# The experts' down products of a mixture-of-experts kernel, each made as two matmuls of 256 columns in place of one of 512

## The reference, cut to what matters

```python
xn = _layernorm(x, axis=-1)
x = x + _L0_attn_ref(xn, ...) + _L0_ffn_ref(xn, Wg, w1, w2)
```

```python
dispatched = xr[dispatch_mask.reshape(-1) % S].reshape(E, C, d)
h = jax.nn.relu(jnp.einsum('ecd,edf->ecf', dispatched, w1))
expert_out = jnp.einsum('ecf,efd->ecd', h, w2)
```

## Time and profile before

| | |
|---|---|
| median of 3 runs | 2025.02 us (2023.58 to 2025.69) |
| span of the profiled execution | 2007.7 us |
| own time of the profiled execution | not given beside its span; the median is 17.3 us over the span |
| PE busy | 1992.3 us, 99% of the span, 11768 matmuls |
| PEld busy | 1648.0 us, 82%, 11768 weight loads |
| DVE, ACT, POOL busy | 897.8, 553.0, 722.7 us |
| granted clock of TensorE | 0.999 of full speed, mean of the span |

### The profile page before, as it was taken

One profiled execution on the slowest core, in us unless ns is written; L12 is line 12 of the kernel. 1 busy time (PEld: TensorE's weight loads), 2 busy tenths in 40 slices (PEclk: granted clock), 3 DMA queues, 4 the chain that ended last, 5 costly groups with the idle time before them and its releaser, 6 DMA issues.

```text
span 2007.7 us, 29146 instructions
## 1 busy us (share of the span) xinstructions
PE 1992.3 (99%) x11768; PEld 1648.0 (82%) x11768; DVE 897.8 (45%) x1792; ACT 553.0 (28%) x986; POOL 722.7 (36%) x600
## 2 busy tenths in 40 slices
PE   9999999999999999999999999999999999999998
PEld 7888888888888888888888888888888888888886
DVE  8777677776842234234323433422242234224311
ACT  6322232223332123124123212411232123123211
POOL 4545453555341324314232331423142324233211
PEclk9999999999999999999999999999999999999999
DMA  6212112111442233316223331621152125224121
GB/s 200 70 64 86 55 54 86 65 66 56 142 131 27 58 75 116 48 48 153 48 64 83 108 50 46 160 41 35 47 161 33 41 49 158 37 61 109 33 33 21
DMA packets 85506, 151.46 MB, mean 75 GB/s; under 512 B 18304, under 2 KB 18304, under 8 KB 85360
## 3 DMA queue, kind: packets, MB, share of 16 engines
q1 hardware_dynamic: 61312, 105.64, 16.2%
q0 software_dynamic: 24048, 43.76, 12.7%
HBM read 109.82 MB, written 39.53 MB: 74 GB/s over the span
## 4 chain that ended last, share of the span: by engine, by line
PE 97%; DVE 1%; SPq 1%; issue 0%; DMA 0%; POOLq 0%; POOL 0%; ACT 0%; DVEq 0%; ACTq 0%
PE bank L1266 48%; PE bank L1570 35%; PE bank L1402 4%; PE bank L1320 2%; PE bank L1625 2%; PE bank L1391 2%; PE bank L1273 1%; PE bank L1385 1%; PE bank L1294 1%; PE bank L1355 1%; PE bank L1365 1%; DMA attn_raw<-in_L_attn_Wv 0%; DVE scores L933 0%; PE bank L1414 0%; SPq L401 0%
## 5 line engine op out<-in xcount | busy, mean ns | idle before, releaser
L1213 DVE SCALAR_TENSOR_TENSOR h_lo<-bank,h_hi 128x512 fp32r<-128x512 f32 x254 | 175.4, 691 | 753.0 <-ACT h_hi L848 752.6
L637 POOL DMA_INDIRECT gathered<-xn_rows,gather_row x304 | 321.4, 1057 | 474.8 <-DVE x_blocks L1068 293.8
L1266 PE MATMUL bank<-xT_hi,w_hi 128*128 128x512 f32 x1024 | 398.8, 389 | 0.0
L1266 PE MATMUL bank<-xT_hi,w_lo 128*128 128x512 f32 x1024 | 398.4, 389 | 0.0
L1266 PE MATMUL bank<-xT_lo,w_hi 128*128 128x512 f32 x1024 | 398.4, 389 | 0.0
L1570 PE MATMUL bank<-w_hi,h_hi 128*128 128x512 f32 x1016 | 395.2, 389 | 0.0
L1570 PE MATMUL bank<-w_lo,h_hi 128*128 128x512 f32 x1016 | 395.2, 389 | 0.0
L1570 PE MATMUL bank<-w_hi,h_lo 128*128 128x512 f32 x1016 | 395.2, 389 | 0.0
L848 ACT ACTIVATE h_hi<-bank 128x512 fp32r<-128x512 f32 x254 | 151.7, 597 | 805.7 <-PE bank L1266 805.5
L650 POOL DMA_INDIRECT out_rows<-y,add_row x80 | 128.9, 1611 | 545.2 <-ACT y L841 472.5
L1266 PEld LDWEIGHTS bank<-xT_hi,w_hi 128*128 128x128 f32 x1024 | 192.2, 188 | 41.6 <-issue 1.3
(11 more groups left out here) (217 smaller groups left out, 2299.7 us busy)
## 6 DMA issues: line engine op xcount, KB each, us to landing
raw_weights<-in_L_ffn_w SPq DMA_DIRECT2D x256, 256.0 KB, 11.3
x_in<-in_L_attn_x SPq DMA_DIRECT2D x32, 256.0 KB, 3.5
xn_rows<-xn SPq DMA_DIRECT2D x32, 256.0 KB, 2.8
x_res<-in_L_attn_x SPq DMA_DIRECT2D x32, 256.0 KB, 4.3
out_rows<-y_attn SPq DMA_DIRECT2D x28, 256.0 KB, 2.0
gathered<-xn_rows,gather_row POOLq DMA_INDIRECT x304, 3.6
out_rows<-y,add_row POOLq DMA_INDIRECT x80, 5.2
attn_raw<-in_L_attn_Wq SPq DMA_DIRECT2D x4, 256.0 KB, 5.2
```

What stands on the lines that cost most here:

```text
L637: pool.indirect_dma_start(xg[:, nth % 2, q * P:(q + 1) * P], None, xn_pieces, bass.IndirectOffsetOnAxis(ap=gather_row[:, col, q:q + 1], ax ...
L1213: v_.scalar_tensor_tensor(lo[:, 0:n * P], h_bank[f % 2][:, 0:n * P], 0.0, hi[:, 0:n * P].bitcast(F32), ALU.max, ALU.subtract).then_inc(S[" ...
L1266: last = mm(dest, at(left[l], t), at_r(right[r], t), start=(i == 0), stop=(i == n - 1))
```

## The change

In `down_part` each matmul over the 512 columns of `y_bank[i]` becomes two, one over the left 256 columns and one over the right 256, with the same stationary operand. The flag `start`, which opens an accumulation in a bank, is set on the very first of the two only; `stop` is set on both of the last. The semaphore `y_done` stands on the last matmul, as before. `up`, the spare blocks and the attention are left as they are.

```diff
                         for l, (hx, wx) in enumerate(((hi, w2_hi), (hi, w2_lo), (lo, w2_hi))):
-                            last = mm(y_bank[i][:, :], hx[:, part], wx[c][:, f % FPC, :],
-                                      start=(f == 0 and l == 0), stop=(f == FT - 1 and l == 2))
+                            for left in (True, False):
+                                half = slice(0, D // 2) if left else slice(D // 2, D)
+                                last = mm(y_bank[i][:, half], hx[:, part], wx[c][:, f % FPC, half],
+                                          start=(f == 0 and l == 0 and left), stop=(f == FT - 1 and l == 2),
+                                          skip_group_check=True)
                         if f == FT - 1:
                             last.then_inc(S["y_done"], 1)
```

## The result

The changed kernel takes 2078.7 us (median of 4 runs, 2076.3 to 2080.7) where the kernel before takes 2025.3 us on the same chip: ratio 1.0264, 95% interval 1.0252 to 1.0276, 53.4 us slower. The forecast was 2032.1 us and a range up to 2068.

The account below looks back on a forecast made before the run. TensorE's matmul stream was taken to bound the kernel: 3072 x 2.3 ns = 7.1 us on the 2007.7 us span, plus 17.3 us from span to median, gave 2032.1 us, range 2014 to 2068 us.

Parts of the forecast that it names:

- The bound, the counts and the rest of the kernel: Whole kernel: one TensorE matmul stream at 2.4 GHz; down gets 6144 matmuls and 6144 loads; other engines do not count.
- the 17.3 us of the median over the span: Whole kernel: median 2025.0 us against span 2007.7 us; the 17.3 us between them were taken to stay.
- The split of the 13.4 ns: Down products: of 13.4 ns above the column steps, 2.3 ns fixed per matmul, 11.1 ns with bytes; +7.1 us.
- rival B: Down products: each matmul pays the full 13.4 ns, a pair takes 240.1 ns; +41 us, 2066 us; chance 0.10 including in-between cases.
- the 112.1 ns of the plain f32 products: Attention: start distance of short f32 products streaming 256 steps, 5.4 ns over the steps; used against a larger fixed part.
- One half's duration: Down products: one matmul of 256 columns should be recorded near 163 + 114 = 277 ns.
- The reading of the earlier trace: 512-column streams with 80-column loads start 230 ns apart, not under 226.7, so load reading beside the stream is unlikely as source.
- rival D: Down products: second load not hidden, +459 us, 2484 us; milder, such as 10 ns per half, +61 us, 2086 us; chance 0.08.
- The load's floor: Down products: full loads overlap and need at most 112 ns each, below the 114.5 ns of a half.
- Issue of instructions: TensorE: 6144 more instructions; small pairs go by in 29 ns against 114 ns per half, so no cost.
- A fall of the clock: Experts' part: the clock should stay full; a fall would make the prediction wrong in a way not costed.
- The `up` products "should stay at 226.7 ns": Experts' part: stretches of up between the down products keep start distances of 226.7 ns, at no cost.

Follow-up runs that it names:

- the second profile of the kernel before: The kernel before, unchanged, profiled once more: span 2007.6 us; on this chip it takes 2010.0 us (9 runs).
- the uneven version: The changed kernel with down products cut into 384 and 128 columns in place of 256 and 256: 2225.1 us against 2029.1 for the kernel before, ratio 1.0968.
- the first kernel of streams: A separate kernel of equal matmuls in streams, by type, columns and load width; fp32r at 256 columns with a full load: 120 ns apart; no total time given.

## Why the prediction was wrong

*The bound, the counts and the rest of the kernel* were right: one stream of TensorE, 6144 matmuls with 6144 loads, nothing moved on the other engines, full clock but for one dip of 3.4 us. One reading beside it was wrong without harm: the 17.3 us of the median over the span are no fixed addition. An execution takes 1.7 us more than its span (2009.35 against 2007.6 us in the second profile of the kernel before); the span of the earlier trace rows agrees with the chip of 2010 us and the median is of the chip of 2025 us.

*The split of the 13.4 ns* is the step that failed: "So a fixed part above 5.4 ns is unlikely. I take 2.3 ns as fixed, and let the other 11.1 ns go with the bytes streamed." With a full load each fp32r matmul pays all of the 13.4 ns, at 256 columns as at 384 and 512; this is rival B, which had a chance of 0.10 with what lies between it and the forecast. It was held to be unlikely for the 112.1 ns of the plain f32 products. Those are another type, which has 2.5 ns on top at 256 and 512 columns, and at 128 columns (256 steps) they run at the floor of their load. That the fit reproduced them (111.8 ns) was a coincidence. One half's duration, forecast at 277 ns from 114 ns of stream, is 283, 6 ns more, and so is the distance.

*The reading of the earlier trace rows* failed too: a shorter load did not shorten a stream of 512, and I took it that the load has no part. At 256 columns it has one, some 6.7 ns of the 13.3. So the milder form of rival D is mixed into B: what is paid by each matmul is shown, and what it is made of is shown in part.

*The load's floor* was right: 112 ns, and it did not bind at 256 columns; at 128 it does, as the uneven version shows. The 109.0 ns of the transposes are no floor for these loads; theirs are recorded at 141 ns, not at 188 to 192.

*Issue of instructions, "This costs nothing"*: it costs 8 us. The argument looked at the rate at which instructions pass, not at how long the 16 or 17 matmuls last that have not started when a branch is taken. *"A fall of the clock"* beside it was the one case named and not costed.

*The `up` products "should stay at 226.7 ns"*: they cost 6.6 us. The kernel before shows such a thing in its attention, distances of up to 236 ns behind the small products, but I had not read it there.

In numbers: 7.1 us forecast; rival B's 41 us, 39 of them in the timeline, and 16 us of which no case spoke. That is why the time lies even above the range.

## What to carry to other kernels

Measure what a matmul has on top of its columns for its own type and its own load before you split it, and don't carry it over from another type. If a stream of TensorE bounds the kernel, take the longest matmuls that the bank allows; two of 256 columns in fp32r cost 13 ns more than one of 512. Look as well at what stands ahead of each jump in the program: the last 16 or 17 matmuls have to last as long as the jump takes, here about 4 us, and what they lack shows as a stall behind it.

## What the runs showed of the hardware

- fp32r matmuls of 512, 384 and 256 columns behind a full load follow each other after 226.7, 173.3 and 120.0 ns, bf16 ones of 512 and 256 after 215.8 and 109.2 ns. The Trainium skill, page "TensorE: Matmul & The Clock Gate", section "Back-to-back issue gap", gives N / 2.4 + 2.5 ns; the bf16 streams agree with it, the fp32r ones do not.
- With 32 columns loaded, fp32r matmuls of 256 columns follow after 113 to 114 ns, with 16 columns loaded after 117 ns, and with a full load after 120 ns; at 512 columns a narrower load brings nothing (229 to 232 ns against 227).
- Full loads of fp32r follow each other after 112 ns at the least in these streams (192, 128 and 64 columns streamed), though a single one is recorded with 188 to 192 ns.
- The stall at a jump depends on the matmuls just ahead of it. Counted beyond the usual distance, the first matmul behind it starts 1.7 to 2.3 us late where fp32r halves stand ahead (four jumps in each version) and 0.0 to 0.6 us where the last 24 are whole. In all versions 16 or 17 matmuls have not started when the first branch is taken, whatever their length and type. The Trainium skill, page "TensorE: Matmul & The Clock Gate", section "Architectural detail: the array is 16× 32×32, not 1× 128×128", says that TensorE's queue holds 64 instructions. That would be 32 pairs of load and matmul, as an estimate 3.8 us of halves; the traces here show about half as many pairs ahead of a branch, 2.0 us of halves. At these stalls the first matmul behind the jump starts 3.8 to 4.4 us after the first branch, so 3.8 us of halves would leave 0.6 us at most.
- The granted clock can fall while TensorE is busy all the time. Windows of a stream with all 128 rows, of one with 64 rows and of one with 32 (us, PE busy, clock):

```profile
100.00:108.00 8.00, 8.00 (x37) 1.00 0.00 0
115.00:125.00 10.00, 10.00 (x47) 0.50 0.00 0
126.00:146.00 20.00, 20.00 (x48) 0.50 0.00 1
```

  The clock fell to 1.2 GHz at 114.2 us, at the end of a first stream of 32 rows (256 columns) that ran without a gap. It stayed there through the stream of 64 rows and the second one of 32 rows (512 columns), and came back in the next stream of full rows. In the first kernel of streams it fell at 56.4 us, in the stream of 64 columns and full rows, 112 ns apart. At 1.2 GHz 512 columns of fp32r took 427 ns (read to the nanosecond), 512 steps with nothing on top.
- The same kernel takes 2010, 2025 or 2029 us on different chips. In the profiles 15 us of difference lie in the attention, in the distances of the small products of lines 1320 and 1365; the cause is open.
